# Hybrid retention, MoE and oscillator kernel: expert regions in DRAM, slots chosen block by block, oscillator tables prepared by ACT

## The chip, the cores and the metric

One NeuronCore of one Trainium2 chip runs the whole program as one launch. The metric is the device time of one execution in microseconds. The kernel before takes 629.99 us, the median of 3 runs (626.58 to 631.67).

## What is computed

A sequence of T = 2048 tokens of width D = 128 goes through four residual branches, all in float32:

```python
x = x + attn_a(layernorm(x))   # 4 layers of retention and MLP
x = x + ffn(layernorm(x))      # shared expert + one of 8 routed experts
x = x + attn_b(layernorm(x))   # oscillator memory: cos(t * freqs), gamma ** t
x = x + ffn(layernorm(x))      # the same weights again
```

The change is in the mixture of experts, and in the tables that the oscillator needs:

```python
shared_out = swiglu(x, shared_gate, shared_up, shared_down)
logits = x @ gate_w.T                       # 8 experts
top_id = argmax(logits); score = sigmoid(max(logits))
routed_out = sum_e swiglu(where(top_id == e, x * score, 0), r_gate[e], r_up[e], r_down[e])
out = shared_out + routed_out               # F = 256 in both

angles = t * freqs                          # the oscillator's tables
decay = gamma ** t
state = (v * cos(angles) + v * k_sh) * g
mem = cumsum(state * decay) / (decay + 1e-6)
```

## The kernel before

The tokens lie in SBUF as `xin`, 16 chunks (NCH) of 128 tokens. The program is four stages after one another: retention (up to 352.9 us of the profiled span), the first call of `ffn` (to 448.4), `oscillator` (to 535.5) and the second call of `ffn` (to 628.8). Between stages all engines meet. Within a stage each engine has one hand-written list of instructions, in the order of the code, and engines wait for each other by semaphores; no scheduler or planner takes part. During the first FFN, `OscillatorTables` adds work to the same lists: decays by doubling on POOL, angles on DVE, sines on ACT.

One call of `ffn` runs so:

- DVE computes mean and scale of every token and the normalised chunks `xn` (L1145). PE first runs 3 matmuls that nobody reads (`keep_running`, L853), then transposes the chunks into 4 PSUM banks (L1045), ACT copies them out, and PE makes the router's logits (L1051) for all 16 chunks.
- DVE chooses the expert of each token for all 16 chunks at once (L1161 to L1168, operands of 128 by 128 elements), PE counts ranks with two matmuls (L1089, L1090), and DVE turns them into a slot for each token (L1198 to L1213). The slots lie densely: an expert's tokens begin at the 128-row tile behind the last tile of the expert before.
- POOL then scatters 16 chunks of scaled tokens (`xs`, L1187) by indirect DMA into `rows_in` in DRAM (L974). Tile t of the 23 tiles (TILES = 16 + 8 - 1) is rows 128t to 128t + 127, and `expert_of` (L1218 to L1221) says whose it is.
- Beside that, the shared expert runs in 4 blocks of 4 chunks: gate and up matmuls of 512 columns on PE (L1059), SiLU on ACT (L998), the product `hs` on DVE (L1175, `shared_hidden`), the down matmuls on PE (L1083), and the sum into `xin` on DVE (L1181, `shared_add`). PE starts block b + 1 before the down matmuls of block b. Then come 3 more matmuls by `keep_running`.
- Then the 23 tiles: SP loads each one (L949, into a ring of 8), PE transposes it (L1111) and multiplies it with the expert's weights (L1119, L1128), which ACT and DVE copy from `routed` by a register read from `expert_of` (L1014, L1234); ACT takes SiLU (L1030), DVE the product (L1249) and the copy `yt` (L1255), and POOL scatters the rows back to the tokens' places (L983).
- In the tail SP gathers `yg` from DRAM in 4 parts (L956), and DVE adds each to `xin` (L1268). In the first call it also takes statistics of it (L1272) and, ahead of these, builds the tables `key_dec` and `out_dec` (`token_decays`, L1919 to L1926). In the second call SP stores the output by blocks (L962).

Before all that, during retention, SP fills `rows_in` of both calls with zeros, one DMA each.

Of the kernel before, what the change touches and what calls it, by code (L numbers as in the profile page):

```python
# [7 lines left out]
ALU = mybir.AluOpType  # L8
# [21 lines left out]
TILES = NCH + EXPERTS - 1  # L30
ROUND = 12582912.0
# [6 lines left out]
def routing_tables():  # L38
# [3 lines left out]
    rows = [EXPERTS - np.arange(EXPERTS), np.arange(TILES),  # L42
            (np.arange(EXPERTS * NCH) % NCH != 0)]
# [48 lines left out]
def build(nc, a, outs):  # L92
    ctx = ExitStack()
    with ctx:
# [9 lines left out]
        small = sb("small", [P, 5 * P + PER_TILE + NCH + EXPERTS + TILES + EXPERTS * NCH])  # L104
# [7 lines left out]
        for name, n in (("earlier", P), ("ones", P), ("rev", EXPERTS), ("tile_no", TILES),  # L112
                        ("restart", EXPERTS * NCH)):
            route[name] = small[:, at:at + n]
            at += n
# [9 lines left out]
        token_ids = sb("token_ids", [P, NCH + TILES], I32)  # L125
        rows_in = [nc.dram_tensor(f"rows_in{n}", (TILES * P, ROW), F32).ap() for n in range(2)]
        rows_back = nc.dram_tensor("rows_back", (T + TILES * P, D), F32).ap()

        ffn_sems = ffn_semaphores(nc, ctx)
        loaded_x = sem("loaded_x")  # L130
# [3 lines left out]
                  loaded_x, loaded_small, ffn_w, rows_in, token_ids, loaded_ffn)  # L134
        tabs = {"cos": sb("cos_tab", [P, 2, T]), "dec": sb("dec_tab", [P, 2, T]),
                "key_dec": sb("key_dec", [P, NCH, 2 * HEADS]), "out_dec": sb("out_dec", [P, NCH, 2 * HEADS])}
# [4 lines left out]
        with ExitStack() as scratch:  # L141
            tables = OscillatorTables(nc, a, tabs, ow, eye, banks, sem, scratch)
# [46 lines left out]
def retention(nc, a, xin, resid, out_stats, consts, small, banks, loaded_x, loaded_small, ffn_w, rows_in,  # L189
              token_ids, loaded_ffn):  # L190
# [11 lines left out]
    with ctx:  # L202
# [11 lines left out]
        rot = sb("rot", [P, 2, NCH, 256])  # L214
# [38 lines left out]
        zero_rows = sb("zero_rows", [P, TILES, ROW])  # L253
# [43 lines left out]
        with nc.Block() as blk:  # L297
            @blk.sync
            def _(sp):
# [20 lines left out]
                sp.dma_start(token_ids[:], a["token_ids"]).then_inc(s["loaded_ids"], 16)  # L320

                sp.wait_ge(s["zeroed"], 4)
# [113 lines left out]
            def _(pool):  # L436
# [34 lines left out]
                run(step)(pool)  # L471

# [383 lines left out]
def ffn_semaphores(nc, ctx):  # L856
    names = ("ones_set", "aggr_done", "rs_chain", "rs_ready", "xn_ready", "xnT_psum",
# [22 lines left out]
def ffn(nc, call, x, stats, w, rows_in, rows_back, token_ids, eye, small, route, banks, loaded_ffn, sems, tables,  # L880
# [8 lines left out]
    with ctx:  # L889
# [10 lines left out]
        hot = sb("hot", [P, EXPERTS, NCH])  # L900
        upto = sb("upto", [P, EXPERTS, NCH])
        place = sb("place", [P, EXPERTS, NCH])
        ntiles, tiles_upto, tiles_before, all_one = (sb(n, [P, EXPERTS]) for n in
# [1089 lines left out]
```

## Time and profile before

| what | value |
|---|---|
| median of 3 runs | 629.99 us (626.58 to 631.67) |
| the profiled execution | 630.61 us |
| its span | 628.8 us, so 1.8 us lie around it |
| granted clock, mean | .936 of 2.4 GHz |
| busy share of the span | PE 86%, PEld 66%, DVE 79%, ACT 55%, POOL 36% |
| POOL indirect scatters into `rows_in` | 32, mean 980 ns |
| zeroing of `rows_in` | 2 DMAs of 1483.5 KB, 14.5 us to landing |

The two FFN calls take 95.5 and 93.3 us of the span. PE's 86% is an average over stages with different limits: in the fronts of the two FFN calls it waits, and what is late there is read from the rows further below, not from the share. PEclk gives the clock granted to TensorE as a share of full speed: 1.0 is 2.4 GHz, and the lower level is 1.2 GHz. Most of its low slices lie in the fronts of the FFN calls and in the oscillator.

### The profile page before, as it was taken

To read this page: it belongs to the slowest core of one execution; us is meant where nothing else is said; L and a number is where in the kernel's file an instruction comes from. 1 tells how busy PE (TensorE), PEld (TensorE's weight loads), DVE (VectorE), ACT (ScalarE), POOL (GpSimd) and SP (SyncE) were. 2 spreads that over 40 slices of the span, in tenths; PEclk is the share of its full clock that TensorE was granted. 3 is DMA by queue.
4 is the path that set the end of the run, shared out by engine and by line. 5 is a ranking of instruction groups with operands and counts; after the bars stand their busy time and mean duration, and the time that the engine had idled before them with its cause. 6 is when DMAs were issued, how large, how long until landed. Compare 5 with 4: busy or idle time off the path is not lost. (4 is left out here: it accounts for less than half of the span.)

```text
span 628.8 us, 13507 instructions
## 1 busy us (share of the span) xinstructions
PE 543.4 (86%) x4308; PEld 415.0 (66%) x4308; DVE 494.0 (79%) x1765; ACT 345.5 (55%) x784; POOL 225.0 (36%) x234
## 2 busy tenths in 40 slices
PE   0787999999999999999976888895299997898990
PEld 0555778788778778877854555795155776555990
DVE  6889988888888888888878783878858999663552
ACT  1545878778777777877744165678034310113770
POOL 3333424424433433433410467565100000063562
PEclk9977999999999999999979679999599999789997
DMA  8919000000000000000000301231200000012225
GB/s 312 373 54 191 7 2 2 1 3 2 2 2 2 2 3 2 3 2 2 2 1 2 109 23 50 57 85 59 59 0 2 1 1 2 0 39 64 64 83 150
DMA packets 32198, 28.54 MB, mean 45 GB/s; under 512 B 4384, under 2 KB 29344, under 8 KB 31872
## 3 DMA queue, kind: packets, MB, share of 16 engines
q1 hardware_dynamic: 27232, 20.69, 11.9%
q0 software_dynamic: 2496, 5.13, 2.5%
q10 hardware_dynamic: 2400, 1.84, 0.9%
q8 instruction: 36, 0.59, 0.4%
q14 instruction: 34, 0.28, 0.1%
HBM read 18.44 MB, written 9.21 MB: 44 GB/s over the span
## 5 line engine op out<-in xcount | busy, mean ns | idle before, releaser
L444 POOL TENSOR_TENSOR att<-att,small 128x512 f32<-128x512 f32 x64 | 82.1, 1283 | 176.6 <-ACT att L347 176.6
L347 ACT ACTIVATE att<-banks 128x512 f32<-128x512 f32 x64 | 38.8, 607 | 49.0 <-PE banks L487 49.0
L355 ACT ACTIVATE xz<-resid,nmr,rs 128x128 f32<-128x128 f32 x128 | 56.6, 502 | 10.9 <-DVE nmr L802 10.9
L983 POOL DMA_INDIRECT rows_back<-ffn_yt,ffn_xt x46 | 46.9, 1020 | 36.7 <-DVE ffn_yt L1255 35.5
L487 PE MATMUL banks<-qexp,qkT 32*128 32x256 f32 x512 | 47.3, 439 | 9.2 <-DVE att L681 9.2
L681 DVE TENSOR_TENSOR att<-banks,small 128x512 f32<-128x512 f32 x64 | 44.0, 688 | 12.0 <-PE banks L487 12.0
L1119 PE MATMUL banks<-ffn_xtT,ffn_wt 128*128 128x128 f32 x368 | 49.8, 278 | 2.9 <-DVE ffn_hr L1249 1.8
L462 POOL TENSOR_TENSOR qk<-cosq,sinq 128x512 f32<-128x512 f32 x32 | 41.0, 1280 | 20.3 <-DVE cosq L730 20.3
L1119 PEld LDWEIGHTS banks<-ffn_xtT,ffn_wt 128*128 128x128 f32 x368 | 44.6, 192 | 4.4 <-ACT ffn_wt L1014 2.7
L853 PE MATMUL banks<-small 128*128 128x512 f32 x38 | 24.2, 791 | 25.7 <-POOL osc_taps L1322 17.8
L503 PE MATMUL banks<-att,ve 128*32 128x128 f32 x1024 | 43.0, 288 | 0.0
L974 POOL DMA_INDIRECT rows_in<-ffn_xs,ffn_slot x32 | 31.3, 980 | 30.6 <-DVE ffn_slot L1213 21.5
L538 PEld LDWEIGHTS banks<-w,hT 128*128 128x128 f32 x256 | 33.4, 204 | 12.6 <-issue 12.5
L538 PE MATMUL banks<-w,hT 128*128 128x128 f32 x256 | 39.7, 302 | 1.8 <-ACT hT L421 1.7
L967 POOL MEMSET ffn_all_one<- 128x8 f32 x2 | 0.2, 104 | 114.0 <-POOLq L1314 84.0
L589 PE MATMUL banks<-xzT,w 128*128 128x256 f32 x128 | 37.1, 414 | 3.1 <-ACT xzT L400 3.1
L723 DVE TENSOR_TENSOR sinq<-banks,rot 128x512 f32<-128x512 f32 x32 | 22.1, 692 | 18.7 <-PE banks L598 18.5
L598 PE MATMUL banks<-wqkvg,xzT 128*128 128x256 f32 x128 | 34.4, 392 | 1.1 <-ACT xzT L400 1.1
L1014 ACT ACTIVATE ffn_wt<-routed_sb 128x512 f32 x46 | 28.9, 630 | 11.0 <-PE banks L1128 9.1
L569 PE MATMUL banks<-small,xz 128*128 128x128 f32 x128 | 21.6, 286 | 14.4 <-ACT xz L355 14.4
L487 PEld LDWEIGHTS banks<-qexp,qkT 32*128 32x128 f32 x512 | 20.8, 189 | 19.4 <-issue 15.8
L1059 PE MATMUL banks<-ffn_xnT,s_gu_sb 128*128 128x512 f32 x64 | 33.4, 673 | 0.0
(249 smaller groups left out, 1430.8 us busy)
## 6 DMA issues: line engine op xcount, KB each, us to landing
rot<-in_rot SPq DMA_DIRECT2D x3, 1024.0 KB, 13.3
routed_sb<-in_routed SPq DMA_DIRECT2D x1, 3072.0 KB, 11.6
rows_in<-zero_rows SPq DMA_DIRECT2D x2, 1483.5 KB, 14.5
ffn_xt<-rows_in SPq DMA_DIRECT2D x46, 64.5 KB, 1.9
ffn_yg<-rows_back SPq DMA_DIRECT2D x8, 256.0 KB, 4.1
rot<-in_rot ACTq DMA_DIRECT2D x1, 1024.0 KB, 10.8
w<-in_W SPq DMA_DIRECT2D x2, 512.0 KB, 7.2
times<-in_times SPq DMA_DIRECT2D x1, 1024.0 KB, 5.1
```

The lines of the kernel that those rows point to most:

```text
L347: act.activation(att[:, c, HALF:HEADS].rearrange("p (r e) n -> p r e n", e=PER_TILE), b_att[:, 2:4, c], ACT.Copy).then_inc(s["att_raw"], 1)
L355: ins = act.activation(xz[:, n], resid[:, (g % GROUPS) * 2 + n % 2], ACT.Identity, scale=rs[:, n:n + 1], bias=nmr[:, n:n + 1])
L444: pool.tensor_tensor(att[:, c, HALF:HEADS], att[:, c, HALF:HEADS], spread(causal.unsqueeze(1), 1, HALF), ALU.mult) \
L462: pool.tensor_tensor(qk[:, v].rearrange("p a b c -> p (a b c)"), cosq[:].rearrange("p a b -> p (a b)"), sinq[:].rearrange("p a b -> p (a b ...
L487: ins = pe.matmul(b_att[:, r, c], qkT[rows, v, 1, c], qexp[rows, v % 2, c], start=True, stop=True)
L503: ins = pe.matmul(out[32 * q:32 * q + 32, :], ve[:, v, c, q, e].rearrange("p j d -> p (j d)"), att[:, c, 2 * q + e, :], start=False, stop= ...
L538: ins = pe.matmul(b_wq[:, c * P:c * P + P], hT[:, f, c * P:c * P + P], w2[:, layer(g), f, :], start=(f == 0), stop=(f == 1))
L589: ins = pe.matmul(b_xv[:, 256 * f:256 * f + 256], w1[:, layer(g), f * P:f * P + P], xzT[:, 2:4], start=True, stop=True)
L598: ins = pe.matmul(b_wq[:, 256 * c:256 * c + 256], xzT[:, c], wqkvg[:, layer(t), 0:2, :], start=True, stop=True)
L681: dve.tensor_tensor(att[:, c, 0:HALF].rearrange("p (r e) n -> p r e n", e=PER_TILE), b_att[:, 0:2, c], spread(spread(causal.unsqueeze(1).u ...
L983: pool.indirect_dma_start(rows_back, bass.IndirectOffsetOnAxis(ap=token, axis=0), yt[:, j % RING], None).then_inc(stored[j % RING], 16)
L1119: ins = pe.matmul(banks[:, 2 + v, n * P:n * P + P], wt[:, j % WT_RING, n * P:n * P + P], xtT[:, v], start=True, stop=True)
```

## The change

Line numbers here are those of the changed kernel unless an L number above is named.

- **Regions.** Each expert gets a region of 2048 rows of its own in `rows_in`. A slot is 2048e plus the token's rank within its expert, so it depends only on earlier tokens, and not on the other experts' totals. `rows_in` grows from 2944 to 17280 rows for each call; it is zeroed by 9 DMAs a call, 18 in all, with 17.8 MB instead of 3.0 MB. The tile's first row is now a number on the chip (`row_of`), which SP reads into a register for each tile.
- **Slots by block.** DVE chooses, counts, scales and places block 0 (4 chunks, operands of 128 by 32), so that POOL can scatter its 4 chunks; then it chooses blocks 1 to 3 in a row, then scales and places each. PE computes ranks by block (5 matmuls each). After that DVE computes the tiles' experts and rows (`tiles_known`), and only then `shared_hidden(0)`.
- **The last shared block** (LATE = 3) moves behind the 23 tiles on PE, ACT and DVE; its sum stands in the tail before part 2.
- **Tables.** ACT does all doublings of `dec`, in pieces between its FFN work, and the angles behind the first SiLU; POOL computes powers of gamma at the end of retention; `token_decays` moves from DVE's tail to behind `shared_hidden(0)`. `cos` and `dec` take the memory of retention's `rot`.
- `keep_running` in front does 2 matmuls instead of 3.

```diff
+SPARE = EXPERTS + TILES - NCH
+ROWS = EXPERTS * T + (SPARE - EXPERTS) * P
...
                 for rows in rows_in:
-                    sp.dma_start(rows.rearrange("(j p) d -> p j d", p=P), zero_rows[:]) \
+                    for e in range(EXPERTS):
+                        sp.dma_start(rows[e * T:e * T + T].rearrange("(j p) d -> p j d", p=P),
+                                     spread(zero_rows[:, e:e + 1], 1, NCH)).then_inc(loaded_ffn, 16)
+                    sp.dma_start(rows[EXPERTS * T:].rearrange("(j p) d -> p j d", p=P), zero_rows[:, EXPERTS:]) \
                       .then_inc(loaded_ffn, 16)
...
                 run(step)(pool)
+                pool.wait_ge(s["rot_ready"], STEPS)
+                tables.one_half(pool)
+                tables.gamma_powers(pool)
...
+                sp.wait_ge(s["expert_ready"], 2)
+
+                def row_at(t):
+                    return sp.value_load(row_of[0:1, t:t + 1], min_val=0, max_val=ROWS - P)
+
+                first_rows = [row_at(t) for t in range(XT_RING)]
                 sp.wait_ge(s["scattered"], 16 * NCH * (call + 1))
...
-                        sp.dma_start(xt[:, v], rows_in[call][t * P:t * P + P, :]).then_inc(x_loaded[v], 16)
+                        sp.dma_start(xt[:, v], rows_in[call][bass.ds(row, P), :]).then_inc(x_loaded[v], 16)
...
-                if tables:
-                    tables.decays(pool)
-                pool.wait_ge(s["slot_ready"], 1)
                 pool.wait_ge(loaded_ffn, 16 * LOADS)
                 for c in range(NCH):
+                    pool.wait_ge(s["slot_ready"], c // BLK + 1)
                     pool.wait_ge(s["xs_ready"], c // BLK + 1)
...
-                if tables:
-                    tables.chunk_powers(pool)
...
+                if tables:
+                    tables.doubled(act, 0, 7)
+                transposed(0)
+                transposed(1)
+                half_angle(0)
+                transposed(2)
+                if tables:
+                    tables.doubled(act, 7, 9)
+                transposed(3)
+                half_angle(1)
+                if tables:
+                    tables.doubled(act, 9, 10)
+                half_angle(2)
+                half_angle(3)
+                if tables:
+                    tables.doubled(act, 10, 11)
...
-                            tables.last_decays(act)
+                            tables.angle(act)
...
                 run(step)(act)
+                shared_silu(LATE)
...
+                def ranks(b):
...
+                    pe.matmul(out, route["earlier"], chunks.rearrange("p c e -> p (c e)"), start=True, stop=False,
+                              skip_group_check=True)
+                    for c in range(BLK - 1):
+                        pe.matmul(out[:, EXPERTS * (c + 1):], route["ones"],
+                                  spread(chunks[:, c:c + 1], 1, BLK - 1 - c), start=False, stop=False,
+                                  skip_group_check=True)
+                    pe.matmul(out, route["ones"], spread(before.unsqueeze(1), 1, BLK), start=False, stop=True,
+                              skip_group_check=True).then_inc(s["ranks_ready"], 1)
...
-                pe.wait_ge(s["shared_added"], NCH // BLK)
+                pe.wait_ge(s["shared_added"], LATE)
                 keep_running(pe, banks[:, 6, :], small, 3)
...
                 run(step)(pe)
+                pe.wait_ge(s["xtT_ready"], TILES)
+                shared_gate(LATE)
+                pe.wait_ge(s["hr_ready"], TILES)
+                shared_up(LATE)
+                shared_down(LATE)
...
-                if tables:
-                    tables.angle(dve)
...
+                for b in range(NCH // BLK):
+                    normalised(b)
+                chosen(0)
+                counted(0)
                 scaled(0)
...
+                placed(0)
+                for b in range(1, NCH // BLK):
+                    chosen(b)
+                    counted(b)
                 for b in range(1, NCH // BLK):
                     scaled(b)
+                    placed(b)
+                tiles_known()
                 shared_hidden(0)
...
+                if tables:
+                    tables.token_decays(dve)
                 if tables:
                     tables.out_weights(dve)
-                for b in range(NCH // BLK):
-                    if b + 1 < NCH // BLK:
+                for b in range(LATE):
+                    if b + 1 < LATE:
                         shared_hidden(b + 1)
                     shared_add(b)
...
-                    tables.token_decays(dve)
+                shared_hidden(LATE)
                 for b in range(NCH // BLK):
+                    if b == 2:
+                        shared_add(LATE)
+                        dve.wait_ge(s["shared_added"], LATE + 1)
```

What `chosen`, `counted`, `placed` and `tiles_known` issue is seen in the rows of order. On DVE, from the first FFN's choice to its slots (`ffn_hot` is the choice as ones and zeros, `ffn_place` the rank masked by it), the kernel before has:

```order
L1161 TENSOR_REDUCE ffn_top_logit<-banks 128x16
L1164 TENSOR_TENSOR ffn_tied<-banks,ffn_top_logit 128x128
L1166 TENSOR_TENSOR ffn_tied<-ffn_tied,small 128x128
L1167 TENSOR_REDUCE ffn_first<-ffn_tied 128x16
L1168 TENSOR_TENSOR ffn_hot<-ffn_first,small 128x128
L1190 COPY ffn_xs<-token_ids 128x16
L1192 TENSOR_SCALAR ffn_score<-ffn_score 128x16
L1187 TENSOR_TENSOR ffn_xs<-ffn_xn,ffn_score 128x4x128
L1198 SCALAR_TENSOR_TENSOR ffn_upto<-small,banks 128x128
```

The changed kernel has there, for block 0, and then from the choice of the next block on:

```order
L1233 TENSOR_REDUCE ffn_top_logit<-banks 128x4
L1235 TENSOR_TENSOR ffn_tied<-banks,ffn_top_logit 128x32
L1236 TENSOR_TENSOR ffn_tied<-ffn_tied,small 128x32
L1237 TENSOR_REDUCE ffn_first<-ffn_tied 128x4
L1238 TENSOR_TENSOR ffn_hot<-ffn_first,small 128x32
L1245 TENSOR_REDUCE ffn_in_block<-ffn_hot 128x8
L1246 TENSOR_TENSOR ffn_count<-small,ffn_in_block 128x8
L1252 TENSOR_SCALAR ffn_score<-ffn_score 128x4
L1253 TENSOR_TENSOR ffn_xs<-ffn_xn,ffn_score 128x4x128
L1260 TENSOR_TENSOR ffn_place<-banks,ffn_hot 128x32
L1261 TENSOR_REDUCE ffn_slot_f<-ffn_place 128x4
L1262 CAST ffn_slot<-ffn_slot_f 128x4
```

These 12 rows stand once for each of the 4 blocks (the first 7 of blocks 1 to 3 in a row, then their last 5), where one list for all chunks stood before. Behind the last slots, up to the first product of the shared expert, DVE has 13 more:

```order
L1267 TENSOR_SCALAR ffn_ntiles<-banks 128x8
L1268 TENSOR_SCALAR ffn_ntiles<-ffn_ntiles 128x8
L1269 TENSOR_SCALAR ffn_ntiles<-ffn_ntiles 128x8
L1270 TENSOR_TENSOR ffn_ntiles<-ffn_ntiles,small 128x8
L1272 TENSOR_SCALAR ffn_skipped<-ffn_ntiles 128x8
L1273 SCALAR_TENSOR_TENSOR ffn_tiles_upto<-ffn_all_one,ffn_ntiles 128x8
L1274 TENSOR_TENSOR ffn_past<-small,ffn_tiles_upto 128x184
L1276 TENSOR_REDUCE ffn_expert_f<-ffn_past 128x23
L1277 TENSOR_SCALAR ffn_expert_of<-ffn_expert_f 128x23
L1279 TENSOR_TENSOR ffn_over<-ffn_past,ffn_skipped 128x184
L1280 TENSOR_REDUCE ffn_row_f<-ffn_over 128x23
```

Two more (`ffn_row_f` and `ffn_row_of`, 128x23) follow, and then `ffn_hs`; before, `ffn_hs` stood right behind the slots and the scaled tokens, and three rows for the experts came after it.

On PE, between the transposes and the shared expert's matmuls (`gate_sb` are the router's weights, `s_gu_sb` the shared gate and up weights), before:

```order
L1045 MATMUL banks<-small,ffn_xn 128x128 x4
L1051 MATMUL banks<-gate_sb,ffn_xnT 128x8 x8
L1089 MATMUL banks<-ffn_hot,small 128x128
L1090 MATMUL banks<-ffn_hot,small 128x128
L1059 MATMUL banks<-ffn_xnT,s_gu_sb 128x512 x4
```

and after, from the last four transposes to the up matmuls of block 0 (the 5 rows of ranks at L1119 to L1125 also stand for block 0 ahead of these, and once more behind the gate matmuls):

```order
L1088 MATMUL banks<-small,ffn_xn 128x128 x4
L1094 MATMUL banks<-gate_sb,ffn_xnT 128x8 x8
L1119 MATMUL banks<-ffn_hot,small 128x32
L1122 MATMUL banks<-ffn_hot,small 128x24
L1122 MATMUL banks<-ffn_hot,small 128x16
L1122 MATMUL banks<-ffn_hot,small 128x8
L1125 MATMUL banks<-ffn_count,small 128x32
L1102 MATMUL banks<-ffn_xnT,s_gu_sb 128x512 x2
...
L1130 MATMUL banks<-ffn_count,small 128x8
L1102 MATMUL banks<-ffn_xnT,s_gu_sb 128x512 x2
```

Gate and up of block 0, 4 matmuls in a row before, are now apart, with the ranks of blocks 2 and 3 and the totals between them, each of which waits for DVE.

## Rows read from the trace of the kernel before

**Rows 1.** Windows, both FFN fronts: us, PE, PEld, DVE, ACT, POOL busy, clock, DMA, GB/s.

```profile
363.40:370.00 6.60, 4.90 (x9) 2.70 (x10) 5.87 (x21) 1.73 (x3) 2.85 (x6) 0.51 0.00 0
548.00:554.80 6.80, 6.36 (x11) 3.26 (x12) 5.93 (x20) 1.02 (x1) 1.21 (x1) 0.51 0.00 0
```

**Rows 2.** Timeline, first FFN, choice to `hs`: start us, us, engine line, [idle before <-releaser].

```profile
356.08 4.23 DVE L1145 TENSOR_SCALAR ffn_xn<-xin,ffn_mv,ffn_rs 128x128 f32<-128x128 f32 x16
...
363.41 0.29 DVE L1161 TENSOR_REDUCE ffn_top_logit<-banks 128x16 f32<-128x128 f32 x1 [0.51 <-PE banks L1051]
...
369.54 0.17 DVE L1213 CAST ffn_slot<-ffn_slot_f 128x16 uint32<-128x16 f32 x1
369.62 1.89 DVE L1187 TENSOR_TENSOR ffn_xs<-ffn_xn,ffn_score 128x512 f32<-128x512 f32 x3
...
370.01 1.36 POOL L974 DMA_INDIRECT rows_in<-ffn_xs,ffn_slot  x1 [3.76 <-DVE ffn_slot L1213]
...
371.90 1.22 DVE L1175 TENSOR_TENSOR ffn_hs<-ffn_sil,banks 128x1024 f32<-128x1024 f32 x1 [0.40 <-PE banks L1059]
```

**Rows 3.** Timeline, first FFN, end of its front.

```profile
389.37 0.96 POOL L974 DMA_INDIRECT rows_in<-ffn_xs,ffn_slot  x1 [0.30 <-issue]
...
390.83 0.69 DVE L1181 TENSOR_TENSOR xin<-xin,banks 128x512 f32<-128x512 f32 x1 [2.21 <-PE banks L1083]
...
391.57 2.84 PE L853 MATMUL banks<-small 128*128 128x512 f32 x6 [0.78 <-DVE xin L1181]
...
391.67 3.65 SPq L949 DMA_DIRECT2D ffn_xt<-rows_in  x8
...
394.25 0.38 PE L1111 MATMUL banks<-small,ffn_xt 128*128 128x128 f32 x2
```

**Rows 4.** Timeline, second FFN, PE and DVE, the same places.

```profile
535.57 5.46 PE L853 MATMUL banks<-small 128*128 128x512 f32 x6 [4.52 <-PEq L1314]
...
544.85 1.91 PE L1051 MATMUL banks<-gate_sb,ffn_xnT 128*128 128x8 f32 x16
...
555.73 1.22 DVE L1175 TENSOR_TENSOR ffn_hs<-ffn_sil,banks 128x1024 f32<-128x1024 f32 x1 [0.88 <-PE banks L1059]
...
560.68 3.60 PE L1059 MATMUL banks<-ffn_xnT,s_gu_sb 128*128 128x512 f32 x8
...
565.90 3.60 PE L1059 MATMUL banks<-ffn_xnT,s_gu_sb 128*128 128x512 f32 x8
...
577.64 0.38 PE L1111 MATMUL banks<-small,ffn_xt 128*128 128x128 f32 x2
```

**Rows 5.** Timeline, first FFN, PE's weight loads around the fall of the clock.

```profile
361.28 1.92 PEld L1051 LDWEIGHTS banks<-gate_sb,ffn_xnT 128*128 128x128 f32 x16
...
365.10 0.50 PEld L1089 LDWEIGHTS banks<-ffn_hot,small 128*128 128x128 f32 x2 [1.89 <-DVE ffn_hot L1168]
```

**Rows 6.** Timeline, DVE in the tails of both calls.

```profile
436.99 0.17 DVE L1919 COPY key_dec<-banks 128x16 f32<-128x16 f32 x1
...
438.88 1.75 DVE L1926 RECIPROCAL out_dec<-out_dec 128x256 f32<-128x256 f32 x1
...
442.05 0.69 DVE L1268 TENSOR_TENSOR xin<-xin,ffn_yg 128x512 f32<-128x512 f32 x1 [1.42 <-DMA ffn_yg<-rows_back]
...
624.48 1.53 DVE L1268 TENSOR_TENSOR xin<-xin,ffn_yg 128x512 f32<-128x512 f32 x2 [1.04 <-DMA ffn_yg<-rows_back]
```

**Rows 7.** DMA issues: out<-in queue, KB each, us from issue to landing.

```profile
rows_in<-zero_rows SPq DMA_DIRECT2D x2, 1483.5 KB, 14.5
```

**Rows 8.** Windows of retention, with the zeroing and without it (columns as in rows 1).

```profile
47.00:62.00 15.00, 11.29 (x103) 7.95 (x104) 14.18 (x46) 7.28 (x19) 6.15 (x5) 0.81 1.15 189
92.00:107.00 15.00, 15.00 (x154) 11.69 (x153) 12.82 (x45) 11.63 (x31) 7.24 (x6) 1.00 0.01 2
```

**Rows 9.** Timeline, retention, POOL and DVE within the first of these windows.

```profile
53.18 1.27 POOL L444 TENSOR_TENSOR att<-att,small 128x512 f32<-128x512 f32 x1 [3.86 <-ACT att L347]
...
53.28 1.21 DVE L159 TENSOR_TENSOR vt<-vt,vv 128x22 f32<-128x22 f32 x1
```

More of the change, by code:

```diff
@@ L909, in ffn @@
         expert_of = sb("expert_of", [P, TILES], I32)
+        over = sb("over", [P, TILES, EXPERTS])
+        row_f = sb("row_f", [P, TILES])
+        row_of = sb("row_of", [P, TILES], I32)
         score = sb("score", [P, NCH])
@@ L988, in _, with transposed @@
             def _(act):
-                for b in range(NCH // 4):
+                def transposed(b):
                     act.wait_ge(s["xnT_psum"], b + 1)
@@ L1073, in _ @@
                 logits(1)
+                ranks(0)
                 transposes(3)
@@ L1085, in shared_down @@
                     ins.then_inc(s["shared_ready"], 1)
-                pe.wait_ge(s["hot_ready"], 1)
-                hot2 = hot[:].rearrange("p e c -> p (e c)")
-                pe.matmul(banks[:, 5, 0:P], route["earlier"], hot2, start=True, stop=True)
-                pe.matmul(banks[:, 5, P:2 * P], route["ones"], hot2, start=True, stop=True) \
-                  .then_inc(s["ranks_ready"], 1)
                 shared_gate(0)
+                ranks(2)
+                ranks(3)
+                counts()
                 shared_up(0)
                 if tables:
+                    pe.wait_ge(s["slot_ready"], NCH // BLK)
                     tables.first_by_token(pe)
-                for b in range(NCH // BLK):
-                    if b + 1 < NCH // BLK:
+                for b in range(LATE):
+                    if b + 1 < LATE:
                         shared_gate(b + 1)
@@ L1836, in last_decays @@
                    .then_inc(self.powers, 1)
-    def double(self, eng, k):
-        dec, n = self.dec, 1 << k
-        eng.wait_ge(self.powers, 2 * k + 2)
-        for f in range(2):
-            eng.tensor_scalar(dec[:, f, n:2 * n], dec[:, f, 0:n], self.gam[:, k, f:f + 1], None,
-                              ALU.mult).then_inc(self.powers, 1)
     def link(self, dve, ins):
@@ L1902 @@
     CHUNK_POWER = 7
-    def chunk_powers(self, pool):
-        row = self.gam_row
-        pool.wait_ge(self.loaded, 16 * self.LOADS)
-        for k in range(self.DOUBLINGS - 1):
-            if k:
-                pool.wait_ge(self.row_squares, k)
-            pool.tensor_tensor(row[:, k + 1], row[:, k], row[:, k], ALU.mult).then_inc(self.row_squares, 1)
     def token_decays(self, dve):
```

270 lines of the change are left out of this document (155 added, 115 removed).

## The prediction

> **What bounds the kernel now.** I read the page's slices first: PE is busy 86%, but the granted clock falls in the fronts of both FFN calls. Windows of these fronts came next, then the timelines of DVE and PE there, then both tails, and last the DMA issues with the retention windows that they fall into.
>
> A front ends where PE transposes tile 0: at 394.25 [rows 3] and 577.64 [rows 4]. Two chains run towards that point. One is the scatter: slots ready at 369.71 [rows 2], 16 scatters from 370.01 to the last, which starts at 389.37, and SP's loads from 391.67 [rows 3]. The other is the shared expert: `hs` of block 0 starts at 371.90 [rows 2], the last sum at 390.83, 3 filler matmuls at 391.57 for 2.84 us [rows 3]. The fillers end when tile 0 starts, and the tile that SP asked for at 391.67 is used without any idle time before the transpose. So the shared chain sets the end; the loads are about as late, but cost nothing visible. From `hs` to tile 0 it takes 22.35 us in the first call [rows 2, 3] and 577.64 - 555.73 = 21.91 in the second [rows 4]. One block's period is 565.90 - 560.68 = 5.22 us [rows 4], with PE nearly always busy in it.
>
> **The change part by part.** *Scatter.* Block 0's slots need 12 DVE instructions instead of 20. These 20 took 369.71 - 363.41 = 6.30 us [rows 2], .31 on average; the nearest rows bound one of mine, a quarter of the elements, by .17 (16 elements) and .29 (128 elements read) [rows 2], and I take .22 with the gap for a 128x32 one and .20 for a 128x8 one. Then choosing costs 5 x .22 = 1.1, counting .22 + .20 = .42, scaling .20 + 1.89/3 [rows 2] with a gap = .92 and placing .22 + .22 + .20 = .64: 3.1 a block. The two angle instructions leave DVE, so the choice starts when `xn` ends, at 356.08 + 4.23 + .2 = 360.5 [rows 2], and the slots of block 0 are there at 363.6, which is 6.1 us earlier. Block 1's come 3 x 1.52 + 1.56 = 6.1 later, longer than POOL needs for 4 scatters at (389.37 - 370.01)/15 = 1.29 each, so the last scatter starts at 369.9 + 11 x 1.29 + 0.3, about 384.2 instead of 389.37. That gain of 5.2 us I cost at nothing: it isn't the chain that ends the front.
>
> *Shared chain up to the first `hs`.* Here the change adds. DVE must do 4 x 3.1 = 12.3 us for slots and 13 instructions of `tiles_known` (9 at .20, 4 larger ones up to .4, together 3.2) before `hs`: 360.5 + 15.5 = 376.0 at the earliest. PE must do ranks for block 0 before the last transposes, then logits, ranks of block 1 (10 records), the gate matmuls (4 records), ranks of blocks 2 and 3 and totals (22 records), then the up matmuls (4 records). The ranks of block 1 end about 4.9 after the first slots: 16 records of logits and 10 of ranks at .2, less what runs beside DVE. Then at the low clock 4 x .91 = 3.6 for gate, at either 22 x .12 = 2.7 or 22 x .25 = 5.5 for ranks, and between 1.8 and 3.6 for up. I take the clock to come back during the gate matmuls for the ranks but to be low again for up: 4.9 + 3.5 + 2.7 + 3.4 + .1 = 14.6 us from the first slots to `hs`. With the high clock all the way DVE's 376.0 is the bound, 12.4 from the slots; with the low one all the way it is about 4.9 + 3.6 + 5.5 + 3.6 = 17.6, less some cover, 16.7. First call: 363.6 + 14.6 = 378.2 instead of 371.90. Second: the first logits come some .3 behind 544.85 [rows 4], the slots at 548.3, `hs` at 562.9 instead of 555.73.
>
> *Three blocks in front.* This takes out one period, 5.22. First call: 22.35 - 5.22 = 17.1, plus .6, because `token_decays`, 438.88 + 1.75 - 436.99 = 3.64 us [rows 6], now delays the second `hs`: 17.7. Tile 0 then starts at 378.2 + 17.7 = 395.9, which is +1.7. Second call: 562.9 + 16.7 = 579.6, +2.0.
>
> *Tails.* In the first call `shared_add`, .69 [rows 3], now stands among DVE's last additions, which run back to back from 442.05 [rows 6] to the end: +.7. Moving `token_decays` out gains nothing, since DVE waited 1.42 us for a DMA there anyhow. In the second call the addition fits into the 1.04 us of idle time at 624.48 [rows 6]. The late gate, up and down matmuls run on PE while the last tiles are scattered and gathered: 0; without that cover 5.2.
>
> *Smaller parts, all taken as 0.* SP's register reads are covered by the wait for the scatter and by the ring of 8 tiles. ACT's doublings stand where ACT was nearly empty (busy 1.73 of 6.60 [rows 1]); without that cover the copies for logits come up to 3 us late. One filler matmul less in front takes 2 x .45 off PE at the high clock, and can cost the rise of the clock. POOL's gamma powers run at the end of retention beside the last layer.
>
> Sum: 1.7 + 2.0 + .7 = +4.4. Against the profiled execution's 630.6 that is 635.0; that run lay .6 above the median of the runs, so against the median the forecast is 634.4.
>
> **The clock once more.** The row shows PE at the low clock after a stretch of short matmuls and waits [rows 1], and the change makes this stretch longer. The Trainium skill (TensorE: Matmul & The Clock Gate, section "HAM oscillation — how this bites in real kernels") says that a PE which works in bursts with pauses between is throttled again each time. By that rule neither front would see the high clock before its second block; the rival below gives this its time, and the trace agrees so far as the filler matmuls at 535.57 ran almost wholly at the low clock [rows 4].
>
> **The rivals.** *The clock stays low through the fronts.* First `hs` 16.7 us behind the slots instead of 14.6: +2.1 in each call, 4.4 + 4.2 = +8.6, median 638.6. For it: the low windows [rows 1] and .91 a record over 5.46 us of unbroken matmuls [rows 4]. Against: 4 records of gate follow closely on the ranks, and PE had the high clock again soon after such a stretch in both calls.
>
> *The clock stays high.* DVE bounds: `hs` at 12.4 behind the slots in the first call, at -.6 in all for tile 0; in the second slots 1.8 earlier and the same 12.4, -2.0; with the tail +.7 this is -1.9, median 628.1. Against it: both fronts fell before, with fewer short matmuls.
>
> *The scatter ends the front after all (the faster side).* If loads that arrive late were what held tile 0 and the fillers only covered it, and the shared chain kept its old start, each front would follow the scatter: -5.2 and in the second call about -5.0, +.7, together -9.5, median 620.5. It decides only if `hs` starts within 1.5 us of where it did, 373.4. Against it stand 61 DVE instructions ahead of it where there were 23.
>
> *The zeroing disturbs retention.* 2 DMAs took 14.5 us each for 3.0 MB [rows 7]; 17.8 MB take about 5.9 times as long, so some 75 us of retention more see full DMA engines. In the window that holds zeroing PE was busy 11.29 of 15.00, in one without it 15.00 of 15.00 [rows 8]. Five more such windows at 3.7 us would be +18.6, the upper bound. But much of the loss has another cause in that window: DVE's 128x22 instruction took 1.21 us while POOL's multiplication ran, 53.28 to 53.18 [rows 9]. I price the disturbance at 1 us a window, +5 on top of the sum: median 639.4. The lower bound is 0, since retention itself moves nothing through DMA then. The Trainium skill (Runtime: NRT & Kernel Launch, section "Instruction fetch mechanics") says that engines stream their instructions in blocks of 16 KiB by a DMA queue of their own; that is the way in which it could hurt, and no row here shows such a wait.
>
> **How the numbers follow.** Chances: forecast .45, clock low .20, clock high .13, zeroing .12, scatter .10. The likeliest one's own range is 632 to 637.5. The range over all goes from 626.5, which leaves the scatter out, to 640.5, which leaves the upper bound of the zeroing and mixtures of both slow rivals out. A measurement here tells 1% from no change: below 623.7 is faster, .10 (the scatter); above 636.3 slower, .20 + .12 and .04 of the forecast's own; the rest, .54, is within 1%.
>
> **What would show it.** Right, if in the changed trace the first scatter starts near 363.9 and the last near 384.2, `hs` near 378 and 563, tile 0 near 396 and 579.6, with the transpose released by PE's own fillers and not by the load. The low clock shows in windows between the first choice and the first `hs` and in gate records of .91. The first call's last addition should end .7 later relative to its first. If retention ends later than 352.9, the zeroing (or POOL's gamma powers) did it. The forecast is wrong if DVE instructions of 32 elements cost no less than those of 128, if PE waits long for DVE between ranks, or if the tile loop's own pace changes, which I take as unchanged.

## The result

The changed kernel takes 634.45 us (median of 16 runs, 629.0 to 638.83), beside 628.7 us (624.97 to 631.91, 16 runs) for the kernel before in the same sessions: ratio 1.0084, 95% interval 1.0056 to 1.0112, so +5.3 us, 3.5 to 7.0. Ratios leave out the runs that lie more than 1.5% above the fastest of their kernel (one of these 16), while medians in microseconds keep them. Its profiled execution took 636.27 us with a span of 634.1. The forecast was 634.4, which is +4.4 on a kernel before of 630.0. That it meets 634.45 so closely is luck: the 16 runs of before have a median 1.3 us below that of the 3 runs that the forecast started from, and the change costs about as much more than was forecast. Not each term came out either.

The stages, each as the difference of two start times in the timelines (front: mean and variance to the transpose of tile 0; loop: to the last `yt` copy; tail: to the next stage or the last addition's end; all us):

| | before | changed | difference |
|---|---|---|---|
| retention, to its end | 352.96 | 352.94 | 0.0 |
| front, first call | 41.29 | 44.49 | +3.2 |
| loop, first call | 39.52 | 38.95 | -.6 |
| last `yt` to first addition | 8.28 | 7.57 | -.7 |
| first addition to oscillator | 6.39 | 7.11 | +.7 |
| oscillator | 87.13 | 87.91 | +.8 |
| front, second call | 42.07 | 42.64 | +.6 |
| loop, second call | 37.05 | 38.51 | +1.5 |
| tail, second call | 11.32 | 10.98 | -.3 |

In the timeline of the changed kernel, first call (start us, us, engine, line), the places that answer to [rows 2, 3]:

```profile
361.35 0.41 PE L1119 MATMUL banks<-ffn_hot,small 128*128 128x32 f32 x2 [0.65 <-DVE ffn_hot L1238]
...
363.13 0.17 DVE L1262 CAST ffn_slot<-ffn_slot_f 128x4 uint32<-128x4 f32 x1
...
364.24 1.19 POOL L994 DMA_INDIRECT rows_in<-ffn_xs,ffn_slot  x1 [11.23 <-DVE ffn_slot L1262]
...
367.85 3.76 PE L1102 MATMUL banks<-ffn_xnT,s_gu_sb 128*128 128x512 f32 x4
371.40 0.47 PE L1119 MATMUL banks<-ffn_hot,small 128*128 128x32 f32 x2
...
373.62 0.19 DVE L1260 TENSOR_TENSOR ffn_place<-banks,ffn_hot 128x32 f32<-128x32 f32 x1 [3.29 <-PE banks L1125]
...
375.95 3.76 PE L1102 MATMUL banks<-ffn_xnT,s_gu_sb 128*128 128x512 f32 x4
...
379.85 1.22 DVE L1289 TENSOR_TENSOR ffn_hs<-ffn_sil,banks 128x1024 f32<-128x1024 f32 x1 [0.37 <-PE banks L1102]
...
384.20 0.96 POOL L994 DMA_INDIRECT rows_in<-ffn_xs,ffn_slot  x1 [0.30 <-issue]
...
397.43 0.38 PE L1175 MATMUL banks<-small,ffn_xt 128*128 128x128 f32 x2
```

The last scatter starts 5.2 us earlier than before, at 384.20, and tile 0 starts 3.2 later, at 397.43. DVE sits idle 3.29 us before it can place block 2, because those ranks stand behind the gate matmuls on PE. `hs` then waits for the up matmuls. Gate and up are four records each and take 3.76 us each, .94 a record: the low clock. Windows of PE and the clock, changed kernel (columns as in rows 1), ten microseconds each, from ten microseconds behind the start of either front:

```profile
362.90:372.90 10.00, 10.00 (x40) 7.93 (x39) 6.53 (x30) 6.87 (x11) 6.83 (x7) 0.53 0.12 36
372.90:382.90 10.00, 10.00 (x29) 6.65 (x30) 7.47 (x29) 4.05 (x3) 7.56 (x9) 0.62 0.17 54
...
549.00:559.00 10.00, 10.00 (x41) 8.22 (x41) 6.54 (x31) 1.37 (x5) 5.82 (x6) 0.55 0.11 34
559.00:569.00 10.00, 8.31 (x40) 5.09 (x40) 6.54 (x23) 1.77 (x2) 7.56 (x9) 1.00 0.15 48
```

From 362.9 to 382.9 PE is busy 10.00 of 10.00 at a clock of .53 and .62: there it does not wait, it works at half speed for most of the time. The same windows of before; the second has the clock at 1.00:

```profile
362.90:372.90 10.00, 8.20 (x22) 4.41 (x22) 8.38 (x24) 4.54 (x6) 5.68 (x9) 0.66 0.02 7
372.90:382.90 10.00, 10.00 (x48) 6.42 (x47) 5.59 (x11) 9.58 (x6) 7.67 (x8) 1.00 0.18 55
```

The second call, the places of [rows 4]:

```profile
549.78 0.17 DVE L1262 CAST ffn_slot<-ffn_slot_f 128x4 uint32<-128x4 f32 x1
...
558.67 0.81 PE L1122 MATMUL banks<-ffn_hot,small 128*128 128x24 f32 x6
...
564.99 1.22 DVE L1289 TENSOR_TENSOR ffn_hs<-ffn_sil,banks 128x1024 f32<-128x1024 f32 x1
...
581.61 0.38 PE L1175 MATMUL banks<-small,ffn_xt 128*128 128x128 f32 x2
```

And the tail of the first call, which answers to [rows 6]:

```profile
443.95 0.69 DVE L1362 TENSOR_TENSOR xin<-xin,ffn_yg 128x512 f32<-128x512 f32 x1 [2.85 <-DMA ffn_yg<-rows_back]
...
446.96 0.67 DVE L1295 TENSOR_TENSOR xin<-xin,banks 128x512 f32<-128x512 f32 x1
```

`shared_add` of the late block stands in a row of additions without idle time and costs its .7.

### The profile page after: what moved, and what is told of

The parts are those of the page before. It is cut to its first block and busy times, and to the rows that moved or that the text cites. A ratio compares the mean times of both kernels' runs of the same rounds, so it can differ in the third digit from the quotient of the medians.

```text
span 634.1 us, 14038 instructions
## 1 busy us (share of the span) xinstructions
PE 559.5 (88%) x4380; PEld 430.0 (68%) x4380; DVE 501.8 (79%) x1835; ACT 354.7 (56%) x810; POOL 211.0 (33%) x216
## 5 line engine op out<-in xcount | busy, mean ns | idle before, releaser
L863 PE MATMUL banks<-small 128*128 128x512 f32 x34 | 22.1, 797 | 18.9 <-POOL osc_taps L1416 11.0
L733 DVE TENSOR_TENSOR sinq<-banks,shared_tab 128x512 f32<-128x512 f32 x32 | 22.1, 692 | 18.8 <-PE banks L608 18.6
L1102 PE MATMUL banks<-ffn_xnT,s_gu_sb 128*128 128x512 f32 x64 | 34.7, 686 | 1.7 <-DVE ffn_hs L1289 1.7
```

The costliest lines, as they stand in the source:

```text
L1102: ins = pe.matmul(banks[:, n, :], w["s_gu"][:, n], rhs, start=True, stop=True)
```

## The experiments

Ratios are to the kernel before, timed beside each.

**zero6: is it the zeroing?** The kernel before with five more DRAM tensors per call, zeroed like `rows_in`.

```diff
-                for rows in rows_in:
+                for rows in rows_in + extra:
```

> The kernel before with six times its zeroing: 10 further DMAs of 1483.5 KB into DRAM tensors that nothing reads, 17.8 MB in all. Theory (retention moves nothing by DMA then, so full DMA engines cost it nothing): retention's end unchanged apart from its scatter between executions, ratio 1.000, within .003. Rival (the zeroing disturbs retention): +5, ratio 1.008, which would be the whole of the change's loss.

Measured: 628.45 us, ratio .9995 (.9963 to 1.0028). The rival of the zeroing, 1.008, falls outside the interval. The retention windows say why; first this kernel, then the changed one:

```profile
92.00:107.00 15.00, 15.00 (x154) 12.19 (x153) 13.40 (x52) 12.34 (x32) 7.49 (x6) 1.00 1.28 182
```

```profile
92.00:107.00 15.00, 15.00 (x154) 11.69 (x153) 12.82 (x45) 11.63 (x31) 7.26 (x6) 1.00 1.27 184
```

The DMA share is 1.28 and 1.27 where it was .01 [rows 8], and PE is busy 15.00 of 15.00 as before. PE's 11.29 in the first window [rows 8] is 11.30 in the changed kernel: it belongs to the place in retention, not to the DMAs.

**regs_in_before: do SP's register reads cost?** The kernel before with each tile's first row from a register.

```diff
+                dve.tensor_scalar(row_of[:], route["tile_no"], float(P), None, ALU.mult).then_inc(s["expert_ready"], 1)
...
-                        sp.dma_start(xt[:, v], rows_in[call][t * P:t * P + P, :]).then_inc(x_loaded[v], 16)
+                        sp.dma_start(xt[:, v], rows_in[call][bass.ds(row, P), :]).then_inc(x_loaded[v], 16)
```

> The kernel before with one part of the change: SP takes each tile's first row from a register, read from a table of 128 t that DVE writes, 8 of them ahead and the rest in the loop; addresses are the same as before. Theory (the reads cost the tile loop of the second call its 1.4 us, by later loads): from tile 0 to the last yt copy 38.3 instead of 37.05 in the second call, sum +1 to +2, ratio 1.002 to 1.003. Rival (regions in DRAM or the shorter front do it): 37.0 and ratio 1.000.

Measured: 629.65, ratio 1.0018 (.9985 to 1.0051): no difference that can be told from none, and the theory's 1.002 to 1.003 lies in the interval as well, so the ratio doesn't decide. Its second loop took 38.24 us, near the 38.3 expected, which looks like the theory; but zero6, whose loop is that of before, shows 38.02, and changed_again below 37.44 with the reads. The loop's length scatters from one execution to the next by more than what was sought, so the theory has no support.

**hs_first: is `tiles_known` ahead of `hs` what hurts?**

```diff
-                tiles_known()
                 shared_hidden(0)
+                tiles_known()
```

> The changed kernel with one edit: DVE runs the first product of the shared expert (hs of block 0) ahead of tiles_known instead of behind it, in both calls. Theory (PE's own work bounds the front, most of it at the low clock; DVE's 13 instructions bind only where the clock is back): in the first call hs of block 0 stays at 379.8, because the up matmuls end at 379.7, and the 3.3 us of tiles_known then push the second hs from 385.85 to about 389, tile 0 +3; in the second call hs moves from 564.99 to 562.8 and tile 0 comes 1 us earlier than 42.6 us behind the front's start. Sum +2, ratio to before about 1.0115. Rival (tiles_known ahead of hs is what makes the change slow): -3.3 in each call, ratio about 0.998.

Measured: 639.41 (median of 10 runs, four of which the ratio leaves out), ratio 1.0113 (1.0067 to 1.016). That is slower than before; whether it is slower than the change too, the overlapping intervals don't tell. The rival, .998, is out. In this trace `hs` of the second call starts at

```profile
567.81 1.22 DVE L1289 TENSOR_TENSOR ffn_hs<-ffn_sil,banks 128x1024 f32<-128x1024 f32 x1 [3.40 <-PE banks L1102]
...
572.08 1.22 DVE L1289 TENSOR_TENSOR ffn_hs<-ffn_sil,banks 128x1024 f32<-128x1024 f32 x1
```

It waited 3.40 us for PE's up matmuls although DVE was free: here DVE's order was not the bound, PE was. This front was 45.69 us instead of some 41.6, since the clock stayed low in it until 568.0, so the part of the theory on the second call wasn't tested.

The first call's front became 47.39 us, +2.9 against the change. That is the size in the theory, but not its way. The first `hs` did not stay where it was: it came 24.03 us behind the front's start (374.14 - 350.11) instead of 26.91, because the clock was high again in the ranks behind the gate matmuls. The second `hs` came at 33.06 instead of 32.91, as good as unmoved, since `tiles_known`, `token_decays` and `out_weights` now all lay between the two. PE had nothing to do meanwhile, and its next records ran at the low clock:

```profile
384.44 3.78 PE L1102 MATMUL banks<-ffn_xnT,s_gu_sb 128*128 128x512 f32 x4 [3.02 <-DVE ffn_hs L1289]
```

So what the early `hs` had gained was lost in that wait, and with the clock at .50 from 383.7 to 390.5 the third `hs` came 1.8 us later behind the front's start than in the changed kernel.

**four_front: does the shared chain set the end?** All four shared blocks in front again; `shared_silu(LATE)`, the late matmuls, `hs` and sum are taken out.

```diff
-        LATE = NCH // BLK - 1
+        LATE = NCH // BLK
```

> The changed kernel with the last shared block back in front of the tiles, in both calls, nothing late. Theory (the shared chain sets the end of the front): tile 0 +5.2 in each call and -.7 in the first call's tail, sum +9.7, ratio 1.024. Rival (the loads behind the scatter set it): 0 in the fronts, -.7 in the tail, ratio 1.007.

Measured: 647.8, ratio 1.0295 (1.0264 to 1.0327). Fronts of 49.71 and 47.69 us: +5.2 and +5.05 against the first trace of the changed kernel, one block's period each, while its last scatter starts 31.27 us behind the front's start, as in the changed kernel (380.88 - 349.61 and 384.20 - 352.94). So the scatter doesn't set the end, and the late block is worth what was said. The median moved 13 us against the changed kernel, more than the 9.7 that the stages explain. The profiled run is the fastest of the four, 644.24; the others, 647.07 to 648.6, had mean granted clocks of .924, .916 and .917 instead of its .926, so the rest goes with a lower clock. What lowered it isn't known.

**keep3: does the third filler matter?**

```diff
-                keep_running(pe, banks[:, 7, :], small, 2)
+                keep_running(pe, banks[:, 7, :], small, 3)
```

> The changed kernel with 3 filler matmuls at the start of each front instead of 2. Theory (the clock bounds): the gate matmuls of block 0, 3.76 us for 4 records in the first call, may get the high clock if the third filler prolongs the unbroken stretch ahead of them, but the clock falls later, in the ranks, so the gain is small: between -2 and +1 in all, ratio 1.005 to 1.010. Rival (the missing filler is why the clock was lost): both fronts keep the high clock, -3 in the first and -2 in the second call, ratio about 1.000.

Measured: 632.01, ratio 1.0046 (1.0026 to 1.0066), just under the theory's band of 1.005 to 1.010, which the interval reaches; the rival's 1.000 is out. Its trace has the first front at 43.26 us, 1.2 shorter than the change's, and the second at 46.35, longer: there the clock was low from 540.2 to 560.7 in spite of the third filler. So this trace doesn't show where the 2.4 us of the medians come from. two_keep2 below takes the filler out of another kernel.

**group_only: are the short records what costs?** Blocks 1 to 3 are chosen and placed as one group of 12 chunks, with an inclusive scan on DVE over the chunks as in the kernel before.

```diff
-                for b in range(1, NCH // BLK):
-                    chosen(b)
-                    counted(b)
-                for b in range(1, NCH // BLK):
-                    scaled(b)
-                    placed(b)
+                chosen_rest()
+                scaled_rest()
+                placed_rest()
                 tiles_known()
                 shared_hidden(0)
...
                 shared_gate(0)
-                ranks(2)
-                ranks(3)
-                counts()
+                ranks_rest()
                 shared_up(0)
```

> The changed kernel with blocks 1 to 3 chosen and placed in one group, and nothing else of two_groups: 2 fillers, tiles_known ahead of the first hs, token_decays where the change put it. Theory (the short matmul records and the DVE instructions by block are what costs): front of the first call about 39.5 us from its start to tile 0 instead of 44.5, of the second about 39 instead of 42.6, ratio .995 to .998. Rival (the order of tiles_known, the decays and the third filler made two_groups fast, not the grouping): fronts within 1.5 us of the changed kernel's, ratio 1.004 to 1.008.

Measured: 629.51, ratio 1.002 (.9984 to 1.0057), between the two. Its fronts, 43.74 and 42.66 us, are within 1.5 us of the first changed trace, as the rival had it: the theory alone was wrong. They don't explain the median, 5 us under the change's, either; in this trace retention ended 3.9 us earlier, at 349.00. The first call's lines:

```profile
370.97 0.17 DVE L1305 CAST ffn_slot<-ffn_slot_f 128x12 uint32<-128x12 f32 x1
...
374.43 1.22 DVE L1331 TENSOR_TENSOR ffn_hs<-ffn_sil,banks 128x1024 f32<-128x1024 f32 x1
```

PE's up matmuls ended at 371.07 here (369.11 and 1.96 us). With PE relieved the bound has moved to DVE: `tiles_known`, 3.3 us between the slots and `hs`, which was hidden behind PE's up matmuls in the changed kernel's first call, is now on the path. PE waits 2.07 us for this `hs` (up to 375.70), and the clock is .50 from 375.9 to 379.4.

**two_groups: both, with the third filler.** group_only, plus `shared_hidden(0)` ahead of `tiles_known`, `token_decays` back in the tail, 3 fillers.

> The changed kernel with blocks 1 to 3 chosen and placed in one group of 12 chunks (operands of 128 by 96, ranks by 4 matmuls instead of 15 and the total), tiles_known behind the first hs, token_decays back in the tail, 3 fillers. Block 0 is still placed alone. Theory (what costs in the front are the 32 short matmul records and the 28 DVE instructions of blocks 1 to 3, by block): slots of chunk 4 at about 373.1 instead of 369.2, last scatter at 387 instead of 384.2, first hs at 375.1 instead of 379.85, tile 0 at 391.8 instead of 397.4, and about the same gain in the second call; sum about -10 against the changed kernel, ratio to before 0.993. Rival (the front is bound by something else, such as the load of the tile after the scatter or the number of shared blocks): tile 0 within 1 us of 397.4, ratio 1.007.

Measured: 624.66, ratio .9923 (.989 to .9956), faster than both kernels. Fronts 38.17 and 37.49 us, 6.3 and 5.2 shorter than the change's. At its first tile in the second call PE waits for something new:

```profile
569.15 0.33 PE L1183 MATMUL banks<-small,ffn_xt 128*128 128x128 f32 x1 [2.10 <-DMA ffn_xt<-rows_in]
```

The shared chain has become shorter than the scatter, whose last DMA starts at 564.31 there. This kernel differs from the changed one in four things, and the runs here split them only in part: grouping alone 1.002 (group_only), with the new places of `tiles_known` and `token_decays` .9957 (two_keep2), with the third filler .9923 and .9884.

**two_groups_again:** the same kernel with more rounds.

> two_groups unchanged, with more rounds. Theory (both fronts 3 to 4.5 us shorter than before, as its trace showed, and nothing else moved): ratio .991 to .995 again. Rival (a lucky draw of the retention stage, which ended between 346 and 353 us in the profiles so far): ratio .997 or more.

Measured: 622.65, ratio .9884 (.984 to .9929). Fronts 38.28 and 37.67. It is faster than before by .7 to 1.6%.

**ranks_first:** in two_groups, `ranks_rest()` stands ahead of `shared_gate(0)`.

> two_groups with the 4 rank matmuls of the group ahead of block 0's gate matmuls instead of behind them. In two_groups tile 0 waited for its load, .75 us in the first and 2.10 us in the second call. Theory (the scatter sets the end there): slots of the group 2 to 3 us earlier, tile 0 .7 earlier in the first and 1.2 in the second call, then bound by the shared chain, ratio .990. Rival (PE idles until DVE has chosen, the gate matmuls and the first hs come later by as much, and the shared chain sets the end again at a later time): fronts +1 each, ratio .995.

Measured: 624.82, ratio .9947 (.9909 to .9985), which alone can't be told from two_groups' .9923. The fronts, 39.43 and 38.95, are 1.3 and 1.5 longer: the rival. PE sat idle until the choice was made, and the clock from 549 to 556 us is .50:

```profile
551.10 0.71 PE L1135 MATMUL banks<-ffn_hotr,small 128*128 128x96 f32 x2 [1.60 <-DVE ffn_hotr L1282]
```

**two_keep2:** two_groups with 2 fillers.

> two_groups with 2 filler matmuls ahead of the transposes instead of 3. Theory (the third filler keeps or brings the high clock for transposes and first logits in most executions, worth about half of what it was worth in keep3, where 1.0084 became 1.0046): ratio .002 above two_groups. Rival (with few short records the filler is of no use and costs its own .9 us a call): ratio .001 to .003 below two_groups.

Measured: 625.81, ratio .9957 (.9934 to .998). The direction is the theory's. The size isn't sharp: .0073 or 4.6 us by the ratio against two_groups_again beside it, 3.2 us by their medians, and .0034 against the ratio of two_groups, where .002 was expected. The traces bear the direction out, with fronts of 40.45 and 40.59 against 38.28 and 37.67. Both second fronts start at 530.43. Windows of two_keep2, then of two_groups_again:

```profile
530.40:540.40 10.00, 9.39 (x40) 6.35 (x41) 9.12 (x51) 1.88 (x4) 0.10 (x1) 0.67 0.00 0
540.40:550.40 10.00, 10.00 (x37) 7.70 (x38) 4.39 (x14) 1.83 (x3) 3.92 (x4) 0.56 0.08 26
```

```profile
530.40:540.40 10.00, 9.71 (x45) 6.35 (x46) 9.11 (x51) 1.89 (x4) 0.10 (x1) 0.74 0.00 0
540.40:550.40 10.00, 10.00 (x42) 6.19 (x42) 7.17 (x22) 1.83 (x3) 4.87 (x5) 0.83 0.08 26
```

One more unread matmul ahead of the transposes, and the clock of the second stretch is .83 instead of .56. The way to the front's end is the scatter: both kernels wait for the first tile's load, two_keep2 so:

```profile
571.02 0.33 PE L1183 MATMUL banks<-small,ffn_xt 128*128 128x128 f32 x1 [2.37 <-DMA ffn_xt<-rows_in]
```

Its last scatter starts at 565.91, the other's at 563.04, 2.87 us apart, and the fronts differ by 2.92.

**changed_again:** the changed kernel once more.

> The changed kernel itself, beside the two others on the same chip. Theory: ratio 1.006 to 1.011 as measured; the fronts of its trace 1 to 3 us longer than before, the second call's tile loop within 37 to 38.9 us as in the other runs. Rival (the 1.4 us of the second call's loop are part of the change): that loop 38.5 again while two_groups shows under 38.

Measured: 635.28, ratio 1.0102 (1.0065 to 1.0138). Fronts 44.48 and 45.67 us, 3.2 and 3.6 longer than before and so just above the 1 to 3 expected; loops 39.64 and 37.44. The second front had the low clock longer than in the first trace; this is what its ranks of blocks 2 and 3 and up matmuls were:

```profile
557.05 0.47 PE L1119 MATMUL banks<-ffn_hot,small 128*128 128x32 f32 x2
557.34 1.43 PE L1122 MATMUL banks<-ffn_hot,small 128*128 128x24 f32 x6
...
561.60 7.44 PE L1102 MATMUL banks<-ffn_xnT,s_gu_sb 128*128 128x512 f32 x12
```

Six records of ranks take 1.43 us here and .81 in the first trace of the same kernel. The second loop is 37.44, within what the theory gave, where the same code took 38.51 in the first trace; zero6 took 38.02 with the loop that took 37.05 in before, and two_groups had 38.92. So the 1.5 us of the table above look like scatter.

## Why the prediction came out

**The scatter.** Right in size and in worth. The first scatter was forecast at 363.9 and started at 364.24, the last at 384.2 (its own terms add up to 384.4) and started at 384.20. The chosen price of .22 us for a 128x32 instruction was good: `placed(0)` at 362.69 to 363.30 took .61. The 5.2 us bought nothing: tile 0's transpose waited for no load, and four_front lengthened the front by a block's period with the scatter where it was.

**From the slots to the first `hs`.** Here a term was mis-sized: "I take the clock to come back during the gate matmuls for the ranks but to be low again for up", 14.6 us. The first call took 379.85 - 363.30 = 16.55, and the trace of changed_again agrees, 16.63. The gate matmuls took 3.76, the 22 records of ranks and totals 375.95 - 371.40 = 4.55 instead of 2.7, and up 3.76. That is the rival with the low clock, which had 16.7 for this. In the second call the ranks did run at the high clock in one trace (564.99 - 549.95 = 15.04); up was then done before DVE was, and DVE's `tiles_known` ended last. In the other trace it took 17.45. hs_first's first call, where the ranks ran at the high clock too, had the 2.7 (372.07 - 369.41 = 2.66) but 1.96 for up: the forecast's mixture, high for the ranks and low again for up, was seen in no front. In the changed kernel's first call DVE waited 3.29, .72 and .37 us for PE; without these waits `hs` would have started at 375.5, near the 376.0 that the forecast gave for DVE alone.

**The clock.** How long the low clock lasts from around the first choice on differs from front to front, and the front's length goes with it. Low stretches (clock .50) and fronts, us:

| | first call: low, front | second call: low, front |
|---|---|---|
| before | 6.8, 41.29 | 6.8, 42.07 |
| zero6 | 6.8, 41.37 | 3.4, 41.18 |
| regs_in_before | 6.8, 41.16 | 10.2, 43.42 |
| changed | 17.1, 44.49 | 10.2, 42.64 |
| changed_again | 17.1, 44.48 | 20.5, 45.67 |
| two_keep2 | 13.7, 40.45 | 10.2, 40.59 |
| two_groups_again | 6.8, 38.28 | 3.4, 37.67 |

In the first call of before and of the changed kernel the clock fell at the same time, 363.5. In before it was high again at 370.3, 4.2 us into gate and up matmuls that follow each other:

```profile
366.11 5.68 PE L1059 MATMUL banks<-ffn_xnT,s_gu_sb 128*128 128x512 f32 x8
```

In the changed kernel the four gate records (367.85, 3.76 us) ended at the low clock, short records followed, and it was high again at 380.6, 4.6 us after up began. In hs_first, with the same instructions on PE, it was high from 370.0, behind the gate records. So the split of gate and up is a plausible reason for the long stretch, but one that no run isolates.

The Trainium skill (TensorE: Matmul & The Clock Gate, "HAM oscillation — how this bites in real kernels") tells of a PE that waits for data between its bursts of matmuls and is throttled again in each wait. The traces agree where PE waits long: during the wait of 3.02 us in hs_first the clock fell, at 383.7. They don't bear it out as the reason here. Before the fall at 363.5 the changed kernel's PE had waited .65 us (361.35), but in before PE was busy 4.00 of 4.00 us from 358.9 to 362.9, and the clock fell at the same time; and through the 17.1 us at .50 in the changed kernel PE was busy for 17.10. So pauses alone don't explain the low clock here, and what else does was not measured.

**Three blocks in front, and the rest of the chain.** Forecast 17.7 and 16.7 us from `hs` to tile 0; measured 397.43 - 379.85 = 17.58 and 581.61 - 564.99 = 16.62. Both right.

**The start of the second front.** The forecast put the choice .3 us behind 544.85, and so the first slots 12.7 us behind the front's start (548.3 - 535.57). But 544.85 is the row of the last 16 records of logits; those of block 0 began at 542.18 in before. Measured 549.95 - 538.97 = 10.98, and 11.32 in changed_again: this term was 1.6 us too long on average.

**Fronts.** +3.2 instead of +1.7 in the first call in both traces of the changed kernel; in the second +.6 and +3.6, where +2.0 stood. The three traces whose fronts have the code of before (before, zero6, and regs_in_before but for one small DVE instruction) give 41.2 to 41.4 and 41.2 to 43.4. With the means of these, 41.27 and 42.22, and of the two changed traces, 44.49 and 44.16, the fronts cost 3.2 + 1.9. That the second comes so near the forecast's +2.0 is luck: its start was 1.6 us too long and its way from the slots to `hs` 1.6 too short (16.2 on average instead of 14.6), and the two traces lie 3 us apart.

**Tails.** Forecast +.7, measured 7.11 - 6.39 = .72 in the first call, and nothing in the second. That with the fronts makes 5.8, inside the measured 3.5 to 7.0. The 4.4 of the forecast was low by the first front's 1.5.

**What the sum did not have.** The profiled executions differ by another +2.2 in the oscillator and the second loop, and by -1.3 in the first loop and up to its first addition. regs_in_before, zero6 and changed_again, with second loops of 38.24, 38.02 and 37.44, show that the loop's part is scatter. For the oscillator's .8 no run separates a cause; in other kernels with the same oscillator it took 86.8 to 88.3 us, before 87.13.

**The rivals.** Zeroing: none to be seen, by zero6, whose interval leaves at most 1.8 us. Scatter as the end: refuted by four_front. High clock throughout: seen in no front. Low clock: true of the first call in both traces, and of the second in one of two; its mechanism was nearer to what ran than the forecast's, though its total, 638.6, was not.

## What to carry to other kernels

Splitting a decision into blocks to start a transfer earlier pays only if that transfer ends the stage; here the last scatter came 5.2 us earlier and nothing waited for it, and the price was dozens of tiny instructions on DVE and PE, ahead of the chain that did set the end, and a longer time of PE at the low clock. Grouping all but the first block kept the early start. By itself that brought 1.002; together with `tiles_known` behind the first `hs`, `token_decays` in the tail and the third filler it was .9923 and .9884. When several chains are nearly level, each edit only moves the bound to the next one: the place of `tiles_known` was free in the first call with the slow PE and cost its 3.3 us with the faster one, so test a reordering again after the edit that relieves the other engine.

## What was not expected of the hardware

- One filler matmul whose result nobody reads, 1.63 us of PE's time in the second call (5.38 and 3.75), was worth 3.2 us by the medians and 4.6 by the ratios (.9884 and .9957), and from 540.4 to 550.4 the clock was .83 instead of .56. It isn't sure: with the third filler, keep3's second front still had the low clock for 20.5 us.
- A wait at the wrong place costs twice. In two_groups_again PE waits 2.34 us for the first tile's load, and two tiles later the eight records of L1191 take 1.92 us where most take 1.06 to 1.22; the clock is .50 from 569.7 to 573.1:

```profile
568.10 0.33 PE L1183 MATMUL banks<-small,ffn_xt 128*128 128x128 f32 x1 [2.34 <-DMA ffn_xt<-rows_in]
...
570.17 1.92 PE L1191 MATMUL banks<-ffn_xtT,ffn_wt 128*128 128x128 f32 x8
```

- Retention, the same instructions on the computing engines in every kernel here but for POOL's few at its end, ended at 346.0 to 353.0 us in the traces. The clock goes with it: from 30 to 346 us it was .96 on average in before, which ended retention at 352.96, and .98 in keep3, which ended it at 346.01. The second front differed by 2.2 us between traces with before's code and by 3.0 between the two of the changed kernel, so a smaller difference between two single traces says little.
